# Transposes and additions of the state sum in pairs, and the fourth group's convolution taps on VectorE

## What is computed

```
# Mamba: 512 channels (d), 16 states (n)
x_in, z = split(x @ W_in)
u   = silu(conv4(x_in) + conv_b)          # depthwise, 4 taps along the tokens
dt, B, C = split(u @ W_xproj);  delta = softplus(dt @ W_dt + b_dt)
h_t = exp(delta_t * A) * h_(t-1) + delta_t * u_t * B_t     # for every d and n
y_t = sum_n C_t[n] * h_t[:, n];  y = (y + D * u) * silu(z);  out = y @ W_out
# experts: router softmax, best 2 of 8, each silu(x@Wg) * (x@Wu) @ Wd, plus a shared expert (2 x 128 wide)
```

## Time and profile before

| | |
|---|---|
| median of 3 runs | 2518.28 us (2516.38 to 2519.62) |
| the profiled execution: device time | 2519.9 us |
| its span, first to last instruction | 2518.1 us |
| granted TensorE clock, mean | 0.887 of full speed |
| busy VectorE (DVE) | 2231.6 us, 89% |
| busy TensorE matmul (PE) | 2151.6 us, 85% |
| busy GpSimd (POOL) | 1934.7 us, 77% |
| busy ScalarE (ACT) | 1677.0 us, 67% |
| first scan starts at | 61.4 us |

### The profile page before, as it was taken

One profiled execution on the slowest core, in us unless ns is written; L12 is line 12 of the kernel. 1 busy time (PEld: TensorE's weight loads), 2 busy tenths in 40 slices (PEclk: granted clock), 3 DMA queues, 4 the chain that ended last, 5 costly groups with the idle time before them and its releaser, 6 DMA issues. The chain is left out here.

```text
span 2518.1 us, 29889 instructions
## 1 busy us (share of the span) xinstructions
PE 2151.6 (85%) x8960; PEld 1374.5 (55%) x8960; DVE 2231.6 (89%) x3192; ACT 1677.0 (67%) x2437; POOL 1934.7 (77%) x1598
## 2 busy tenths in 40 slices
PE   5578989889898988989889898988989898896878
PEld 2345565556555555555645555565555556564554
DVE  2899998999999999999999999999999999988961
ACT  4556776677667767777676777667767676764532
POOL 3577887978778797878879788797878879686843
PEclk8758989999899899989889898998989898997979
DMA  4111211111112111111211221121112111111201
GB/s 120 38 34 43 63 55 48 56 56 52 49 59 61 47 54 52 59 51 56 63 47 45 61 60 51 55 64 43 47 51 68 51 56 55 43 51 42 63 22 42
DMA packets 92945, 134.25 MB, mean 53 GB/s; under 512 B 12000, under 2 KB 42976, under 8 KB 92784
## 3 DMA queue, kind: packets, MB, share of 16 engines
q1 hardware_dynamic: 92784, 132.34, 17.4%
HBM read 123.13 MB, written 9.18 MB: 53 GB/s over the span
## 5 line engine op out<-in xcount | busy, mean ns | idle before, releaser
L757 DVE TENSOR_TENSOR_SCAN h<-d_a,carry,d_bu 128x512 f32<-128x512 f32 x1024 | 1290.9, 1273 | 60.7 <-ACT d_a L599 60.7
L1002 POOL TENSOR_TENSOR d_bu<-delta_u,b_rows 128x1024 f32<-128x1024 f32 x512 | 1201.4, 2360 | 5.0 <-DMA b_rows<-b_rows_hbm 0.5
L599 ACT ACTIVATE d_a<-delta,a_neg 128x512 f32<-128x512 f32 x1024 | 696.4, 689 | 573.3 <-DVE h L757 571.1
L447 PE MATMUL ht<-ident,h 128*128 128x128 f32 x4096 | 700.6, 303 | 275.5 <-DVE y_t L767 263.2
L447 PEld LDWEIGHTS ht<-ident,h 128*128 128x128 f32 x4096 | 533.3, 154 | 668.8 <-DVE y_t L767 351.8
L767 DVE SCALAR_TENSOR_TENSOR y_t<-ht,c_t,y_t 128x512 f32<-128x512 f32 x960 | 694.0, 733 | 47.6 <-PE ht L447 46.5
L1065 POOL TENSOR_TENSOR hidden<-silu_gate,up 128x512 f32<-128x512 f32 x160 | 203.8, 1274 | 211.5 <-ACT up L669 115.4
L509 PE MATMUL ring<-x_t,w_gate_sb 128*128 128x512 f32 x640 | 354.5, 684 | 1.1 <-ACT x_t L656 1.0
L516 PE MATMUL ring<-x_t,w_up_sb 128*128 128x512 f32 x640 | 312.3, 613 | 0.0
L536 PE MATMUL dn<-w_down_sb,hidden 128*128 128x256 f32 x1280 | 303.0, 380 | 1.3 <-POOL hidden L1070 1.3
L536 PEld LDWEIGHTS dn<-w_down_sb,hidden 128*128 128x128 f32 x1280 | 231.3, 190 | 30.9 <-issue 3.1
(11 more groups left out here) (110 smaller groups left out, 2003.1 us busy)
## 6 DMA issues: line engine op xcount, KB each, us to landing
b_rows<-b_rows_hbm SPq DMA_DIRECT2D x256, 256.0 KB, 3.5
coef_rows<-coef_rows_hbm SPq DMA_DIRECT2D x128, 256.0 KB, 3.5
xa<-L_attn_x_in SPq DMA_DIRECT2D x16, 512.0 KB, 3.9
xr<-L_attn_x_in SPq DMA_DIRECT2D x16, 512.0 KB, 3.9
out<-xr SPq DMA_DIRECT2D x16, 512.0 KB, 3.1
w_in_sb<-L_attn_W_in_in SPq DMA_DIRECT2D x1, 1024.0 KB, 6.4
w_gate_sb<-L_ffn_experts_gate_in SPq DMA_DIRECT2D x2, 512.0 KB, 4.7
w_up_sb<-L_ffn_experts_up_in SPq DMA_DIRECT2D x2, 512.0 KB, 5.5
```

What stands on the lines that cost most here:

```text
L447: last = nc.tensor.transpose(HT[q % HTS][:, j * P:(j + 1) * P], H[:, (NS * c + n) % HS, j, a * P:(a + 1) * P], IDN[:, :])
L599: nc.scalar.activation(DA[i % DAS][:, :], DL[:, r, j, :], ACT.Exp, scale=ANEG[:, j, n:n + 1]).then_inc(ex.sem, 1)
L757: nc.vector.tensor_tensor_scan(H[:, (NS * s + n) % HS, j, :], DA[(n * J + j) % DAS][:, :], BU[:, (2 * n + j // 2) % 4, j % 2, :], CARRY[:, ...
L1002: nc.gpsimd.tensor_tensor(BU[:, (2 * n + h) % 4, :, :], DU[:, 2 * h:2 * h + 2, :], BB[:, n % 2, :].unsqueeze(1).to_broadcast([P, 2, T]), A ...
```

## The change

1. TensorE transposes two quarters at a time, at the head of every odd slot: quarters t-5 and t-4 in slot t. VectorE adds two at a time after the scan of every even slot: t-6 and t-5 in slot t (the first state's quarters stay with ScalarE). `LATER` is gone.
2. The last quarters: 58 and 59 are added at the end of slot 63, 60 and 61 in slot 0 and 62 and 63 in slot 1 of the next body. In slot 0 the residual of two chunks back (`add_stream_y`) now stands ahead of the additions.
3. The tables follow. What comes behind the last addition is one slot sooner (YD_PE, YD_DVE, Y_GATE, OUT_PE, O_STATS, X1_STATS, X1T_PE; XIN_PE, TAP0_ACT and CONV too, with TAP0_ACT of groups 2 and 3 in slot 8). ROUTE_DVE, ROUTE_EXP, CT_PE, DL_PE, DL_ACT, XA_STATS and XA_RSTD are one slot later. The second to fourth pair of expert blocks start at 22, 32, 42 in place of 21, 31, 41. Silu of u, groups 2 and 3, is in slot 11 in place of 12.
4. The fourth group's taps are made as the others': VectorE makes head and three taps in slot 11. ScalarE's three scaled taps, GpSimd's three additions and the semaphores `scaled` and `conv_last` are gone.

```diff
-        XIN_PE, TAP0_ACT, CONV = (5, 5, 8, 9), (5, 6, 9, 9), (7, 8, 11, 11)
-        POOL_J, POOL_CONV = J - 1, 11
-        YD_PE, YD_DVE, Y_GATE, OUT_PE = 3, 4, 5, (6, 6, 7, 7)
-        O_STATS, X1_STATS, X1T_PE = 9, 10, 11
-        PAIR_AT = (12, 21, 31, 41, 50)
-        ROUTER_PE, ROUTE_DVE, ROUTE_EXP = 14, (15, 17, 18), 15
-        XD_PE, CF_PE, CT_PE = 18, 20, 47
-        DL_PE, DL_ACT = (27, 28, 37, 38), (29, 29, 39, 39)
-        XA_STATS, XA_RSTD, XA_NORM = (31, 31, 41, 41), 43, 49
+        XIN_PE, TAP0_ACT, CONV = (4, 4, 7, 8), (4, 5, 8, 8), (6, 7, 10, 11)
+        YD_PE, YD_DVE, Y_GATE, OUT_PE = 2, 3, 4, (5, 5, 6, 6)
+        O_STATS, X1_STATS, X1T_PE = 8, 9, 10
+        PAIR_AT = (12, 22, 32, 42, 50)
+        ROUTER_PE, ROUTE_DVE, ROUTE_EXP = 14, (16, 18, 19), 16
+        XD_PE, CF_PE, CT_PE = 18, 20, 48
+        DL_PE, DL_ACT = (28, 29, 38, 39), (30, 30, 40, 40)
+        XA_STATS, XA_RSTD, XA_NORM = (32, 32, 42, 42), 44, 49
...
-        SILU = {8: [("u", 0), ("u", 1)], 12: [("u", 2), ("u", 3)], 58: [("z", 0), ("z", 1)], 62: [("z", 2), ("z", 3)]}
-
-        LATER = {13: 16, 22: 25, 28: 31, 32: 35, 42: 45, 51: 54}
-        ADDS, todo = {}, iter(range(NT, SLOTS))
-        for t in range(2 * NT + 1, SLOTS):
-            count = 0 if t in LATER else 2 if t in LATER.values() else 1
-            ADDS[t] = [next(todo) for _ in range(count)]
+        SILU = {8: [("u", 0), ("u", 1)], 11: [("u", 2), ("u", 3)], 58: [("z", 0), ("z", 1)], 62: [("z", 2), ("z", 3)]}
+
+        ADDS = {t: (t - NT - 2, t - NT - 1) for t in range(NT + 2, SLOTS, 2)}
+        ADDS[SLOTS] = (SLOTS - NT - 2, SLOTS - NT - 1)
+        ADDS_LATE = {0: (SLOTS - NT, SLOTS - NT + 1), 1: (SLOTS - NT + 2, SLOTS - NT + 3)}
...
                 for t in range(SLOTS):
-                    if with_scan and t >= NT:
-                        transpose_state(s, t - NT)
-                    if ffn and t < NT // 2:
-                        transpose_state(s - 1, SLOTS - NT + 2 * t)
-                        transpose_state(s - 1, SLOTS - NT + 2 * t + 1)
+                    for q in ADDS.get(t + 1, ()):
+                        if with_scan:
+                            transpose_state(s, q)
+                    for q in ADDS_LATE.get(t, ()):
+                        if ffn:
+                            transpose_state(s - 1, q)
...
-                        if j == POOL_J:
-                            act.wait_ge(o_full.sem, o_full.at(c - 2))
-                            act.wait_ge(conv_last.sem, conv_last.at(c - 1))
-                            for k in range(TAPS - 1):
-                                back = TAPS - 1 - k
-                                nc.scalar.activation(YD[:, k, back:], ring_bank("xin", j)[:, 0:T - back], ACT.Copy,
-                                                     scale=CW[:, j, k:k + 1]).then_inc(scaled.sem, 1)
...
-                    if with_scan and t in ADDS:
-                        for q in ADDS[t]:
+                    if exists(lo - 2) and t == 0:
+                        for a in range(NT):
+                            add_stream_y(s - 2, a)
+                    for q in ADDS.get(t, ()):
+                        if with_scan and q >= NT:
                             add_state(s, r, q)
+                    if with_scan and t == SLOTS - 1:
+                        for q in ADDS[SLOTS]:
+                            add_state(s, r, q)
+                    for q in ADDS_LATE.get(t, ()):
+                        if ffn:
+                            add_state(s - 1, o, q)
...
-            def add_taps(c, o, j):
-
-                for i in range(TAPS - 1):
-                    k = TAPS - 2 - i
-                    back = TAPS - 1 - k
-                    pool.wait_ge(scaled.sem, scaled.at(c))
-                    pool.wait_ge(conv_last.sem, conv_last.at(c, i + 1))
-                    nc.gpsimd.tensor_tensor(U[:, o, j, back:], U[:, o, j, back:], YD[:, k, back:], ALU.add)\
-                      .then_inc(conv_last.sem, 1)
```

More of the change, by code:

```diff
@@ L161, in mamba_moe_kernel @@
         xd, ct = stage("xd_s", 1), stage("ct_s", 1)
-        tap0, scaled = stage("tap0", J), stage("scaled", TAPS - 1)
+        tap0 = stage("tap0", J)
         shift = {w: stage(f"shift_{w}", n) for w, n in dict(xa=2, o=1, x1=2, y=3).items()}
@@ L821, in body @@
                                 moments_end("xa", s + 2)
-                    if ffn and t == 0:
-                        add_state(s - 1, o, SLOTS - NT - 1)
-                    if exists(lo - 2) and t == 0:
-                        for a in range(NT):
-                            add_stream_y(s - 2, a)
-                    if ffn and t in (1, 2):
-                        for a in (2 * t - 2, 2 * t - 1):
-                            add_state(s - 1, o, SLOTS - NT + a)
             def over(t):
@@ L874, in route, with ffn_part @@
                 last.then_inc(rt.sem, 1)
-            def ffn_part(c, o, t, prepared):
+            def ffn_part(c, o, t):
                 if t == YD_DVE:
                     for j in range(J):
-                        skip_u(c, o, j, prepared)
+                        skip_u(c, o, j)
                 if t == O_STATS:
@@ L903, in ffn_part @@
                     moments_end("y", c)
-            def conv_head(c, o, j, done):
-                dve.wait_ge(tap0.sem, tap0.at(c, j + 1))
-                dve.wait_ge(head.sem, head.at(c))
-                nc.vector.scalar_tensor_tensor(U[:, o, j, 0:TAPS - 1], ring_bank("xin", j)[:, 0:TAPS - 1],
-                                               CW[:, j, TAPS - 1:], HEAD[:, j, :],
-                                               ALU.mult, ALU.add).then_inc(done.sem, 1)
-            def conv_part(c, o, t):
-                if t == CONV[POOL_J]:
-                    dve.wait_ge(scaled.sem, scaled.at(c))
-                    conv_head(c, o, POOL_J, conv_last)
-                for j in range(POOL_J):
-                    if t == CONV[j]:
-                        conv_head(c, o, j, conv)
-                        for i in range(TAPS - 1):
-                            k = TAPS - 2 - i
-                            back = TAPS - 1 - k
-                            dve.wait_ge(conv.sem, conv.at(c, TAPS * j + i + 1))
-                            nc.vector.scalar_tensor_tensor(U[:, o, j, back:], ring_bank("xin", j)[:, 0:T - back],
-                                                           CW[:, j, k:k + 1], U[:, o, j, back:],
-                                                           ALU.mult, ALU.add).then_inc(conv.sem, 1)
@@ new lines, in conv_part @@
+            def conv_part(c, o, t):
+                for j in range(J):
+                    for i in range(TAPS - 1):
+                        if t != CONV[j]:
+                            continue
+                        bank = ring_bank("xin", j)
+                        if i == 0:
+                            dve.wait_ge(tap0.sem, tap0.at(c, j + 1))
+                            dve.wait_ge(head.sem, head.at(c))
+                            nc.vector.scalar_tensor_tensor(U[:, o, j, 0:TAPS - 1], bank[:, 0:TAPS - 1],
+                                                           CW[:, j, TAPS - 1:], HEAD[:, j, :],
+                                                           ALU.mult, ALU.add).then_inc(conv.sem, 1)
+                        k = TAPS - 2 - i
+                        back = TAPS - 1 - k
+                        dve.wait_ge(conv.sem, conv.at(c, TAPS * j + i + 1))
+                        nc.vector.scalar_tensor_tensor(U[:, o, j, back:], bank[:, 0:T - back], CW[:, j, k:k + 1],
+                                                       U[:, o, j, back:], ALU.mult, ALU.add)\
+                          .then_inc(conv.sem, 1)
@@ L1025, in body @@
                         rstd_of("x1", s - 1)
-                    if prep and t == POOL_CONV:
-                        add_taps(s + 1, o, POOL_J)
                     if exists(lo + 2) and t == XA_RSTD:
```

16 lines of the change are left out of this document (4 added, 12 removed).

## The result

The changed kernel takes 2461.7 us (median; 2459.6 to 2462.4) against 2518.0 for the kernel before: ratio 0.9775, 95% interval 0.9758 to 0.9792. The profiled execution took 2459.6 with a span of 2457.8, 60 less than that of before.

The account below looks back on a forecast made before the run. VectorE was taken to set the pace. Terms 35 - 33 + 3 - 22 - 3 + 7 - 3 = -16 took the profiled 2519.9 to 2504, so 2502 for the median; range 2476 to 2536.

Parts of the forecast that it names:

- signs that it named for being wrong: A decay wait over 1 us in slots 11 to 17, additions' waits over 2.5 a chunk, or mean granted clock under 0.87.
- best case: Rival in which no half clock meets a burst and the third pair wins 2.4 a chunk: 2481 us, chance 0.12.
- VectorE paces, and only its waits can be won: VectorE, busy 139.4 of 148.5 us a chunk, sets the pace; its 7.9 us of waits are nearly all reordering can win.
- Three taps, +2.3 a chunk: The fourth group's three taps on VectorE cost 2.3 us a chunk, all on the path: +35 us over 15 chunks.
- Worth nothing inside: Taking 1.83 us off ScalarE and 4.08 us off GpSimd frees engines with spare time, so wins nothing inside.
- Slots 9 to 16: Waits for scan 15's decay (1.58) and the router (0.95) fall from 2.5 to 0.3 us a chunk: -33 us.
- The router's part: Router stays in slot 14, its reader moves to 16, giving more room; winning only this 0.95 us wait would be -14.
- Table swaps: At the gates' silus in slots 24, 34, 44, 52, about 0.2 us is lost each, against three places before: +3 us.
- TensorE's burst at the third pair: VectorE's waits in slots 35 to 38 fall from 2.4 to 0.9 us a chunk: -22 us, bounds 0 and -36.
- Last burst: Slots 50 to 60: TensorE's 19.5 us stand against VectorE's 17.3, leaving 2.2 of waiting: -3 us.
- Other stalls, +7: Longer, rarer TensorE idle time may put a half-clock stretch on the second or fourth pair: 0.5 us a chunk, bounds 0 and +1.8.
- Terms put at nothing: Moves said to cost nothing: last additions and all behind them one slot sooner, SP's transfers, GpSimd's order; no term for the rest.

## Why the forecast was right in direction and short in size

The forecast was 2502, with a range from 2476 to 2536; measured were 2461.7. None of the signs that it named for being wrong came up, and even its best case, 2481, was 19 too slow.

- **VectorE paces, and only its waits can be won**: right. The run with added work shows the full price, and waits, overlaps, taps and scans add up to the 39.9 of the 15 chunks.
- **Three taps, +2.3 a chunk**: right (x192, 143.7 us as forecast). That the old order gives 10 of the 35 back, and the new order all 35, was not foreseen. "Worth nothing inside" was wrong for the new order: with the scaled taps on ScalarE and the silu as late as GpSimd's additions ask, scans wait 2.0 us more a chunk.
- **Slots 9 to 16**: the decay's part right in mechanism and size (1.58 before, nothing after; the walk's "just fits" is 0.2 us of room; undoing it costs 20). The router's part right in size by luck, and wrong in cause: moving its reader did nothing.
- **Table swaps**: right, four waits of 0.19 each for the decay, and 0.85 and 1.5 where one or two additions of cover are taken away. From the first load at 1096.49 to the decay at 1100.25, load, two silus and load take 3.76, which is 1.28 + 1.15 + 1.28 and 0.05 between them. The Trainium skill (ScalarE: Activation LUTs, "What ACT_TABLE_LOAD costs") gives 1283 ns for the load and 2.66 us for a switch with its drain. The trace agrees with the first and shows no drain: 3.76 holds two switches.
- **TensorE's burst at the third pair**: the step that failed. The waits of additions there were put at 2.4 before and 0.9 after, by pairs and by the place of the statistics; they went to nothing, and by neither. The prediction held that the lead would be the same afterwards and that the idle time ahead of the pair would remain, and priced what the half clock does. That idle time was a wait for an addition, listed as such in the earlier trace rows, which `LATER` had put off, and the change removed `LATER`: one entry of that table, taken out of the kernel before, gives 34 us. Without it 0.80 us is left of 0.55 and 1.18, and does no harm. And 6.8 us at half clock cost 0.4 in the run with single quarters, without `LATER`, not the 1.8 that the prediction gave them for pairs. It should have asked, of every entry of the table that goes, whose wait it was.
- **Last burst**: put at 2.2 of waiting, measured 2.71 and 0.2, so 15 x 0.7 = 11 us on the other side. The burst was counted as nine pieces and nine quarters, 19.5 us, from the end of the additions of slot 50. It has ten quarters (slots 51 to 59), and the first pair starts 0.35 us after those additions, behind a gate. TensorE's timeline, the first pair and what follows the last down:

```profile
1176.62 1.04 PE L442 MATMUL ht<-ident,h 128*128 128x128 f32 x8
1196.48 1.88 PE L548 MATMUL ring<-z_buf,w_in_sb 128*128 128x512 f32 x4
```

  These are 19.9 us, without idle time between. The prediction's 1.73 for a gate, up or down stands in none of its rows (the rows that it names show 3.62 at half clock and 1.89 for a down); the distances between starts bear it out, 1.72 from 1177.49 to 1179.21, where the first down begins.
- **Other stalls, +7**: none. TensorE's idle time as a whole is no less (span less busy time: 366 us before, 374 after), but it lies in fewer pieces: transposes waited for additions 285 times, 263 us, and now 116 times, 147 us, and the mean clock went up from 0.887 to 0.924. The Trainium skill (TensorE: Matmul & The Clock Gate, "A second HAM failure mode: psum-queue depth-cycling") blames frequent short pauses between groups of matmuls for a swinging clock. Fewer pauses and a higher clock agree with it, though no run here changes the one without the rest. That pairs would bring more half clock was wrong.
- **Terms put at nothing.** Overlaps and shorter scans, 15 us, were in no term, nor was the tail. Nor was a wait of the last chunk: in slot 9 of before it waited for the output projection as no other chunk does, since without convolutions VectorE arrives early. Before, then after (VectorE's statistics and, of before, TensorE ahead of the projection):

```profile
2297.42 1.63 DVE L779 BATCH_NORM_STATS2 stats_o<-dn 128x6 f32<-128x256 f32 x4 [6.79 <-PE dn L471]
```
```profile
2287.32 1.11 PE L447 MATMUL ht<-ident,h 128*128 128x128 f32 x4 [3.11 <-ACT y_t L607]
2288.22 6.13 PE L471 MATMUL dn<-w_out_sb,y_d 128*128 128x256 f32 x16
```
```profile
2245.07 1.63 DVE L763 BATCH_NORM_STATS2 stats_o<-dn 128x6 f32<-128x256 f32 x4 [1.72 <-PE dn L466]
```

A single quarter's transposes stood between x_in and the projection and waited 3.11 us for ScalarE's copy of the first state; the projection behind it then ran at half clock. In the new order the four parts of the projection stand together ahead of those transposes. The last chunk takes 143.2 to 145.1 us in all four kernels of the old order and 131.6 to 134.9 in all with even pairs, so its gain belongs to the order. Of its 11.7 us only 5 are this wait; additions and router give the rest, and these are already in the factor of 15, since the first chunk that is scanned has nothing behind it and the last one has.

Together, for the whole run. Waits are VectorE's, over all 16 chunks and without the first scan's own:

| | forecast | measured |
|---|---|---|
| the fourth group's taps | +35 | +36 |
| additions that wait for transposes (third pair, other stalls) | -15 | -41 (46.0 to 5.4) |
| scans that wait for the decay, and the router (slots 9 to 16, swaps) | -30 | -38 (39.3 to 17.2, and 15.6 to 0) |
| statistics of slot 60 (last burst) | -3 | +11 (27.8 to 39.1) |
| statistics of slot 9, heads, GpSimd's reciprocal root | 0 | -6 (9.1 to 1.7, 3.2 to 0.5, 0 to 4.5) |
| overlaps of waits, shorter scans | 0 | -15 |
| lead-in | -3 | -6 |
| tail | 0 | -3 |
| sum | -16 | -60 |

The additions' waits are the largest miss, 26 of 44 us. The 15 are what is left of VectorE's busy time, 21 more, after the taps' 36; fewer waits and the scans account for 13 of them.

## What to carry to other kernels

When a hand-written order is replaced by a regular one, price each exception that goes by the wait it causes on other engines, not only by the one it was made for; one put-off addition cost 34 us here. Where two function tables alternate on ScalarE, count the work that the pacing engine has between the last result before the swap and the first needed after it; one addition of 0.64 us more or less shows in full, in every chunk. Multiply by the right number of rounds, and look at the first and last round by themselves.

## What was not expected of the hardware

Where the clock falls to half changes with small things: with 2.3 us more on VectorE a chunk, the stretch at half clock ahead of the third pair shrank from 6.8 to 3.4 us and every chunk became alike (150.2 us), where before 147.4 and 149.6 took turns. With one quarter in every slot that stretch is 6.8 us in two chunks of one and the same execution, 3.4 in five and absent in seven. A part of a change that costs 35 us by itself measured 25 inside, and 20 with its lead-in. And the lead-in of the same code varies: the first scan started at 58.6, 60.4 and 61.4 us in three kernels that differ only in `LATER`.
